# Shared-expert steps of a mixture-of-experts layer: all sixteen in the routing stage

## The reference

```python
logits = flat @ router_w
_, topk_idx = jax.lax.top_k(logits + router_bias, K)
...                       # softmax shares of the four experts: comb
g = jax.nn.silu(jnp.einsum('nd,edf->nef', flat, wg))
u = jnp.einsum('nd,edf->nef', flat, wu)
routed = jnp.einsum('ne,nef,efd->nd', comb, g * u, wd)
sg = jax.nn.silu(jnp.einsum('nd,sdh->nsh', flat, swg))
su = jnp.einsum('nd,sdh->nsh', flat, swu)
shared = jnp.einsum('nsh,shd->nd', sg * su, swd)
return (routed + shared).reshape(b, t, d)
```

## Time and profile before

| | |
|---|---|
| median of 3 runs | 1293.5 us (1292.83 to 1296.53) |
| the profiled execution | 1294.35 us |
| its span, first to last instruction | 1292.6 us |
| mean granted clock of TensorE, share of full speed | 0.929 |
| PE, DVE, ACT, POOL busy | 1117.1, 867.2, 615.2, 407.7 us |
| routing stage | from about 234 us |
| expert stage | 361.5 to 496 us |
| mid stage | 496 to about 656 us |

### The profile page before, as it was taken

How to read it: one execution, slowest core, us unless ns; L and a number is a source line. 1 busy time by engine, 2 the same in 40 slices (tenths; PEclk the granted TensorE clock), 3 DMA queues, 4 the chain that set the end, 5 groups by cost and what they waited for, 6 DMA issues and landing times. The chain is left out here.

```text
span 1292.6 us, 31608 instructions
## 1 busy us (share of the span) xinstructions
PE 1117.1 (86%) x12162; PEld 916.7 (71%) x12162; DVE 867.2 (67%) x2172; ACT 615.2 (48%) x1404; POOL 407.7 (32%) x592
## 2 busy tenths in 40 slices
PE   5569998547689997777779999999999999999987
PEld 4446776445478996665547888888888888888776
DVE  5467997757646766688556667666766686664565
ACT  4434455222234443466735554555455555553654
POOL 3331122067700455784038005400530152000221
PEclk9879999757889998888789999999999999999999
DMA  6747785222289884354233334233352342232001
GB/s 161 182 125 203 215 230 185 98 74 90 93 330 417 292 280 164 104 177 143 87 108 110 94 95 143 85 85 105 124 156 85 112 118 91 84 103 84 1 17 50
DMA packets 78562, 177.74 MB, mean 138 GB/s; under 512 B 12678, under 2 KB 26246, under 8 KB 75846
## 3 DMA queue, kind: packets, MB, share of 16 engines
q1 hardware_dynamic: 72140, 158.67, 38.6%
q0 software_dynamic: 6272, 17.05, 4.4%
HBM read 114.40 MB, written 61.08 MB: 136 GB/s over the span
## 5 line engine op out<-in xcount | busy, mean ns | idle before, releaser
L2318 ACT ACTIVATE decay<-masked,negcum 128x128 f32<-128x128 f32 x512 | 163.1, 391 | 102.8 <-DVE mixT L2382 102.8
L2226 PE MATMUL joint<-xh,w_high 128*128 128x512 f32 x512 | 209.3, 409 | 2.0 <-POOL wl L2162 2.0
L2226 PE MATMUL joint<-xl,w_high 128*128 128x512 f32 x512 | 200.2, 391 | 0.0
L2226 PE MATMUL joint<-xh,wl 128*128 128x512 f32 x512 | 199.9, 390 | 0.0
L2430 DVE COPY cT<-joint 128x512 f32<-128x512 f32 x128 | 88.3, 690 | 86.0 <-PE joint L2226 85.7
L2336 ACT ACTIVATE bT<-joint 128x512 f32<-128x512 f32 x128 | 76.6, 599 | 129.9 <-PE joint L2226 129.9
L2382 DVE TENSOR_TENSOR mixT<-pcb,decay 128x512 f32<-128x512 f32 x128 | 82.4, 685 | 57.8 <-PE pcb L2242 57.8
L2159 POOL TENSOR_TENSOR w_high<-w_in,none 128x512 fp32r<-128x512 f32 x32 | 37.0, 1155 | 260.4 <-DMA w_in<-in_w_bc 250.0
L2226 PEld LDWEIGHTS joint<-xh,w_high 128*128 128x128 f32 x512 | 96.2, 188 | 23.6 <-POOL wl L2162 2.4
L2226 PEld LDWEIGHTS joint<-xh,wl 128*128 128x128 f32 x512 | 96.1, 188 | 20.8
L2226 PEld LDWEIGHTS joint<-xl,w_high 128*128 128x128 f32 x512 | 96.3, 188 | 17.0
(11 more groups left out here) (373 smaller groups left out, 2715.7 us busy)
## 6 DMA issues: line engine op xcount, KB each, us to landing
cumrow<-ssm_cum SPq DMA_DIRECT2D x128, 256.0 KB, 3.3
slots_in<-blank SPq DMA_DIRECT2D x16, 1024.0 KB, 5.6
rows<-slots_in SPq DMA_DIRECT2D x32, 512.0 KB, 5.1
slots_out<-spare SPq DMA_DIRECT2D x32, 512.0 KB, 3.8
weights<-in_expert_quads SPq DMA_DIRECT2D x16, 768.0 KB, 9.1
w_in<-in_w_bc SPq DMA_DIRECT2D x32, 256.0 KB, 3.7
qk_parts<-parts SPq DMA_DIRECT2D x32, 192.0 KB, 2.3
stack<-qk_parts SPq DMA_DIRECT2D x32, 192.0 KB, 5.4
```

The source lines that it names most:

```text
L2226: last = nc.tensor.matmul(bank[:], w[:, j, col:col + P], a[:, k, c * CHUNK:(c + 1) * CHUNK], start=(m == 0), stop=(m == len(parts) - 1))
L2318: last = nc.scalar.activation(decay[:, n % 2, o], masked[:, n % 2, o], ACT.Exp, bias=negcum[:, c * TPC + i, head:head + 1])
```

## The change

`LATE`, `NOW` and everything with `late` go. `stage_route` runs all 16 steps (`STEPS = SHARED * NCH`). The four steps of chunk 0 now stand between the ranking of chunk 1 and the turning of chunk 2, which waits for chunk 0's `take` since `turned` uses the banks of `acc`. The other twelve follow the routing of chunk 3. DVE's half of a step is cut in two, `product` and `low`, and the pieces are put between other work; `find_slots` takes a function that it calls after its last MAX. In `stage_mid` nothing of the steps is left, and `first` becomes (0, 2, 2, 0). The transfers of `late_raw` and the splitting of the shared weights in the mid stage are gone.

```diff
-    STEPS = SHARED * NOW
+    STEPS = SHARED * NCH
...
                 place_chunk(0)
                 place_chunk(1)
+                pe.wait_ge(logits_out, EARLY_NORMS)
+                for n in range(SHARED):
+                    up(n)
+                    if n:
+                        down(n - 1)
+                down(SHARED - 1)
+                pe.wait_ge(y_out, 1)
                 turn(2)
+                turn(3)
                 score(2)
-                turn(3)
                 score(3)
                 place_chunk(2)
                 place_chunk(3)
                 pe.wait_ge(logits_out, NCH)
...
+                for n in range(SHARED, STEPS):
+                    up(n)
+                    if n > SHARED:
+                        down(n - 1)
...
+                step(0)
+                step(1)
+                fill_rows(2)
+                step(2)
+                fill_rows(3)
+                step(3)
+                take(0)
+                high_parts(2)
+                high_parts(3)
+                for n in range(SHARED, STEPS):
+                    step(n)
...
                 find_slots(0)
+                step(0)
                 statistics(x, OF_X, 2)
                 add(3)
+                step(1)
                 statistics(x, OF_X, 3)
-                find_slots(1)
+                product(2)
+                find_slots(1, lambda: low(2))
+                step(3)
                 low_parts(2)
+                low_parts(3)
                 choose(2)
-                low_parts(3)
                 choose(3)
                 tables(1)
-                find_slots(2)
-                step(0)
-                find_slots(3)
-                step(1)
+                product(4)
+                find_slots(2, lambda: low(4))
+                product(5)
+                find_slots(3, lambda: low(5))
+                product(6)
                 find_owners()
+                low(6)
...
+                for k in range(TOPK):
+                    product(10 + k)
+                    link(nc.vector.tensor_tensor(moved[:], place[:],
+                                                 last4[:, :, k:k + 1].broadcast_to([P, NT, NE]), ALU.is_equal))
+                    low(10 + k)
+                    link(nc.vector.tensor_tensor(moved[:], moved[:], expd[:], ALU.mult))
+                    link(nc.vector.tensor_reduce(share[:, :, k], moved[:], AX.X, ALU.add))
+                for n in range(10 + TOPK, STEPS):
                     step(n)
...
-                    if i + DEEP == NQ:
-                        for s in range(SHARED):
-                            sp.dma_start(t["late_raw"][s], ins["shared_w"][:, s, :]).then_inc(t["late_loaded"], 16)
...
-                    first = (2, 2, 2, 0)[g]
+                    first = (0, 2, 2, 0)[g]
...
-                for n in range(LATE_STEPS):
-                    late_step(n)
-                late_down(LATE_STEPS - 1)
                 pe.wait_ge(split_done, 2)
                 turn(0)
...
-                late_step(1)
-                late_step(2)
-                combine_two(0)
-                late_step(3)
-                late_step(4)
-                combine_two(2)
-                dve.wait_ge(added, TPC * TOPK)
-                late_step(5)
+                combine(0)
                 statistics(y, OF_Y, 0)
-                late_step(6)
-                late_step(7)
                 add(0)
                 statistics(x, OF_X, 0)
                 low_parts(0)
```

More of the change, by code:

```diff
@@ L1012, in place_chunk, with hidden, up, down @@
                     rank(g)
+                def hidden(bank, s, col, c, done):
+                    tok = slice(c * CHUNK, (c + 1) * CHUNK)
+                    terms = [(w, a, k) for k in range(KD) for w, a in ((sh, xh), (sh, xl), (sl, xh))]
+                    for m, (w, a, k) in enumerate(terms):
+                        last = nc.tensor.matmul(bank[:], w[:, s, col + k * P:col + (k + 1) * P], a[:, k, tok],
+                                                start=(m == 0), stop=(m == len(terms) - 1))
+                    last.then_inc(done, 1)
+                def up(n):
+                    c, s = n // SHARED, n % SHARED
+                    if n >= 2:
+                        pe.wait_ge(silu_done, n - 1)
+                    hidden(pg[n % 2], s, 0, c, gate_done)
+                    if n:
+                        pe.wait_ge(prod_done, n)
+                    hidden(pu, s, D, c, up_done)
+                def down(n):
+                    c, s = n // SHARED, n % SHARED
+                    pe.wait_ge(lo_done, n + 1)
+                    if s == 0 and c:
+                        pe.wait_ge(y_out, c)
+                    for i in range(TPC):
+                        for m, (a, w) in enumerate(((hh, sh), (hh, sl), (hl, sh))):
+                            last = nc.tensor.matmul(acc[i // 2][:, i % 2, :], a[:, n % 2, i * P:(i + 1) * P],
+                                                    w[:, s, 2 * D:3 * D], start=(s == 0 and m == 0 and i % 2 == 0),
+                                                    stop=(s == SHARED - 1 and m == 2), skip_group_check=True)
+                    last.then_inc(down_done, 1)
                 turn(0)
@@ L1026, in _ @@
                 pe.wait_ge(logits_out, NCH)
[L1028 to L1048, removed]
-                    for s in range(SHARED):
-                        if not (first and s < 2):
-                            pe.wait_ge(silu_done, c * SHARED + (s - 1))
-                        hidden(pg[s % 2], s, 0, c, gate_done)
-                        after(pe, prod_done, c * SHARED + s)
-                        hidden(pu, s, D, c, up_done)
-                        if s:
-                            down(c, s - 1)
-                        elif not first:
-                            down(c - 1, SHARED - 1)
-                repeat(pe, NOW, body)
+                for n in range(SHARED, STEPS):
+                    up(n)
+                    if n > SHARED:
+                        down(n - 1)
                 pe.wait_ge(owner_found, 1)
@@ L1105, in take, with step @@
                     last.then_inc(y_out, 1)
-                for n in range(STEPS):
+                def step(n):
                     act.wait_ge(gate_done, n + 1)
@@ L1241, in step @@
                                             ALU.subtract).then_inc(lo_done, 1)
+                def step(n):
+                    product(n)
+                    low(n)
                 statistics(y, OF_Y, 2)
@@ L1476, in stage_mid @@
     val = t["val"].rearrange("p v (t n) -> p v t n", n=P)
-    sh, sl, l_gate, prod, hh, hl = (t["late"][n] for n in ("sh", "sl", "gate", "prod", "hh", "hl"))
     with ExitStack() as ctx:
```

137 lines of the change are left out of this document (20 added, 117 removed).

## The result

| | median, us | runs from, to | ratio to the kernel before |
| --- | --- | --- | --- |
| before | 1293.17 | 1288.37 to 1296.53 (9 runs) | |
| changed | 1298.01 | 1295.20 to 1304.86 (9 runs) | 1.0047, 95% interval 1.0027 to 1.0068 |

The changed kernel is slower by 0.47%, some 6 us with an interval of 3.5 to 8.8. (The ratio is taken over all runs; the quotient of the two medians is 1.0037.) Predicted were 1301.5 and a range of 1295 to 1306. The profiled execution of the changed kernel took 1295.2 us, the fastest of its nine; that of before took 1294.35. So the two traces differ by 0.85 us where the medians differ by 4.8: the stages must be compared, each from its own first instruction, not the two spans.

A forecast was written before the change was run, and what follows sets the result against it. POOL was taken as the bound, by its scatters in routing and gathers in the mid stage. Terms 3.5 + 0.7 - 0.3 + 4.1 = +8.0 on the profiled 1294.35 us, less 0.85 to the median, gave 1301.5 us, range 1295 to 1306.

The forecast's parts named there:

- third term: Mid stage: POOL idles before the first deviations, 6.2 us less 2.1 for shorter gathers, +4.1 us.
- rival 1: Routing stage: PE's clock is up when chunk 2 is turned, so its slots are not delayed; 1298 us, chance 0.18.
- First term: Routing stage: at the lower clock chunk 2's slots come late and delay POOL's scatters, +3.5 us.
- Second term: Routing stage: scatters from chunk 2 on are lengthened by six more VectorE low parts, +0.7 us.
- The steps hidden: Routing stage: steps 4 to 15 end before SP's issues do, with some 3.5 us to spare; nothing added.
- Rival 2: Routing stage: the step chain outlasts the scatters and the stage ends 3.4 us later; 1305 us, chance 0.12.
- Expert stage: Expert stage: four issues and 1.5 MB leave SP's queue near its end, -0.3 us.
- rival 3: Mid stage: gathers speed up without the late steps, keeping chunk 0's 4.5 us head start; 1291.4 or 1289 us, chance 0.10.
- Rival 4: Whole kernel: no change to speak of, routing terms nothing and gathers gaining some 3 us; 1295 us, chance 0.12.
- theory A: Stated with the experiments: the loss is POOL's mid-stage idle time (`first`); the moved steps cost about what they give.

The follow-up runs named there:

- e2: The changed kernel with `first` = (2, 2, 2, 0) as before, so two gathers ahead again; 1292.22 us, 0.9997.
- e5: e2 with `find_slots(2)` straight behind `tables(1)`, ahead of product 4 and its low part; 1292.45 us, 0.9997.
- e6: e2 with three groups of six filler matmuls on PE, into banks that nothing reads; 1289.95 us, 0.9979.
- e9: The kernel of e6 once more, run beside e10; 1290.51 us, 0.9997.
- e1: The changed kernel once more, with no edit; 1297.84 us, 1.0048.
- e8: The changed kernel with `first` = (1, 2, 2, 0), one gather ahead; 1293.47 us, 1.0005.
- e3: The kernel before without the mid stage's eight late steps and the shared weights' second load and splitting, part of the output left out; 1289.03 us, 0.9976.
- e4: e3 with `first` = (0, 2, 2, 0) as in the change, the same part of the output left out; 1297.36 us, 1.0044.
- e7: e3 with 22 VectorE subtractions of 128 x 512 in SBUF added beside the gathers of chunks 0 and 1; 1292.60 us, 1.0001.
- e10: The kernel of e2 once more, run beside e9; 1289.63 us, 0.9999.

## Why the prediction was right, point by point

The direction was right, and so was the third term as the largest; the time was 3.5 us too high. The mechanism of the mid stage was the one predicted, and the sizes of three terms were off. Luck has a part in it: the median of 1298.01 lies just outside the forecast's own range (1298.5 to 1304.5) and is the number of rival 1 (1298), and the changed kernel's trace shows that rival's mechanism. Two signs that the prediction named for being right didn't show (chunk 2's first scatter at 307.32 and not about 313, the first transpose at 360.53 and not near 365.7), and one that it named for being wrong did (scores at 0.11 us). The stated range was wide enough for both accounts.

- **First term** (chunk 2's slots late, predicted +3.5 with bounds 0 and +4). This is the step that was mis-sized most. The working was right for an execution with the low clock: e2 shows the wait of 5.87 us and +4.55. But it was priced as if every execution ran so, since the scores of the kernel before did. In the five profiles with the routing stage of the change as it is, the low clock stands once, in e2. The mean start of chunk 2 is +49.5 there and +48.5 in the four with the old order, so the term is about +1.0, and nearly all of it is that one execution. (e5, e6 and e9 had the full clock too, but e6 and e9 have matmuls added to that very end, so they don't count for how often it stands.) In e1 and e8 POOL waited 1.6 us for the slots with the scores at 0.11, so the 8 us of slack are gone at the full clock as well. In the changed kernel's own profile it is 0: rival 1. "TensorE: Matmul & The Clock Gate" of the Trainium skill (Part 1: The HAM clock gate) says that the throttled state is the default and that activity releases it. If chunk 0's work was enough to release it, that rule, which I set aside for the row of the same scores, gave 0 for this term; four of the five traces agree with it and e2 doesn't.
- **Second term** (scatters lengthened by the added low parts, predicted +0.7, bounds 0 and 1.2). From chunk 2's start to the last scatter the means are 47.6 and 46.1: +1.5, above my upper bound of 1.2 (the five as they are give 47.3, so +1.2). The mean scatter takes 1122 ns in the eight and 1067 in the four, 1.8 us over 32 of them. I counted the low parts alone, not the products nor the last shares that now stand there too; that these are the reason is argued, not tested. Together the two terms made some +2.3 where I had +4.2.
- **The steps hidden.** Right: `take` ended at 355.5, before SP's loads at 356.47. Counted from the first scatter that is 4.2 us sooner than I had it; which of the steps were quicker I didn't follow up. Rival 2 did not happen. `find_slots(1)` was hidden too: chunk 1's first scatter waits for nothing on DVE.
- **Expert stage** (-0.3). From PE's first transpose to the first gather: 135.24 us where it was 135.84. The second load of the shared weights stands in the kernel before alone, as e3, e4 and e7 leave it out too; the mean of the eleven profiles without it is 135.7, in a spread from 134.7 to 136.9. So no gain can be told from this spread.
- **Third term** (+4.1: 6.2 of idle time less 2.1 of shorter gathers). The idle time was right to 0.1 us: 7.09 for 7.2, behind the combination and the statistics that I had named. The shortening was 3.5 and not 2.1, so the stage's last gather moved by 3.3 and its end by 2.7. Its place was wrong in part. The 1.0 for the eight gathers beside the combination came out (0.9). The 1.1 for splits and products beside the first 16 was there (the second and third gather took 1.37 and 1.42 us before and 0.96 and 0.95 after), but two gathers beside DVE's work on the weights of the state-space projection took 1.74 and 2.16 before and 1.90 and 2.99 after, so that the 16 together stayed at 18.6 and 18.5. In its place 2.5 us went in the 40 gathers behind, which I had left alone except in the bound. With `first` unchanged and no late steps, the 64 gathers take 0.9 to 3.8 us less than before (e2, e3, e5, e6, e9 and e10), and the mid stage is 3.4 us shorter. e7 shows that VectorE work from SBUF to SBUF is enough for such a loss; how the late steps caused theirs, beyond the wait of 0.94 us, stays open. The price of `first` alone was right: 7.2 - 1.0 = 6.2 by the working, 6.05 at the last gather between e2 and the change, 6.4 between e3 and e4, 5.9 in the length of the stage.
- **Rivals 3 and 4.** Gathers did speed up, but from chunk 1 on only from 1.40 to 1.33 us in the mean with the gap of 0.30, above the 1.3 from which rival 3 was to decide. Its lowest time was also added up wrongly: 1293.5 - 1 + 4.1 - 6.6 is 1290.0 and not 1289, so its chance of 0.07 below 1289.6 had no sum behind it. Rival 4 had 3 us for the gathers, about what they gained in all (3.5), but with 3 in all its terms give 1296.4; its 1295 needs the 3 on top of the third term's 2.1. And routing cost more than nothing.

In medians: taking out the late steps gives 3 us (e3), running them in routing costs them back (e2 and e10 are level with before), and `first` adds 5.6 (e1 less e2). The profiles agree: routing is 2.2 us longer in the five with the routing stage of the change than in the four with the old one (from the first scatter to PE's first transpose), leaving out the late steps saves 3.4 in the mid stage, and `first` adds 5.9. So theory A holds: within the 2.5 us or so that these runs resolve, the whole of the measured loss is `first`, and 38 us of PE work moved between two stages bound by POOL came to nothing.

None of the versions is resolved as faster than the kernel before while doing all of its work: e2 and e10 tie with it, and e6's lead did not repeat. What stays open is how often the low clock meets the scores in the changed order: one in five profiles is too few to tell. The other runs don't show it: each has only one mean clock for its whole span. Of the kernel before, the slowest of the 34 beside e1 (1296.42 us) had 0.925 and the fastest (1285.95) 0.933, so part of the spread goes with the clock, but not where in the program.

## What to carry to other kernels

Moving work off a stage gains only what it took from that stage's bound: here 38 us of PE work went from one stage bound by POOL to another, and the time stayed level. Leaving the late work out altogether was worth 3 us, and 22 VectorE operations put in its place cost as much. When a queue issues transfers for the next chunk ahead of a step that waits on the present one, those few issues cover the wait; taking them away shows at full price. And a term that hangs on TensorE's clock should be priced at both levels with a chance for each, when the new order differs from the old in how PE's waits fall, instead of from the old order's clock.

## What the runs showed of the hardware

- One program, two clocks. e2 and e10 are the same code. The matmul behind product 2 started at the same point after the first scatter in both (13.05 and 13.04 us). In e10 PE had done the work ahead of it partly at the low clock (0.71 from 260 to 265, PE busy throughout) and then waited 1.41 us; in e2 it had done it at full clock (1.00, PE busy 4.25 of 5 us), was through sooner, waited 2.96, and that matmul took 0.79 us instead of 0.51. The engine that had been faster ended at the lower clock, and the chunk behind it 5.2 us later.
- A gather of 128 rows mostly takes POOL 0.95 us and a gap of 0.30, and 1.15 us beside subtractions of 0.69 us on VectorE from SBUF to SBUF. 22 of them (e7) made the first 24 gathers 2.1 us longer than in e3 and the stage 3.4.
- A gather beside a long VectorE operation in SBUF ends only after it: 2.99 us beside a subtraction of 2.56 (changed kernel), 0.82 behind its end. Which gather is caught can change from one execution to the next: the 36th took 2.47 us in e2 and 1.28 in e10, the same code.
